# Eight columns of a graph kernel's edge lists: from one-hot products to GpSimd gathers

## The chip, the cores and the metric

The kernel runs on one core of a Trainium2 chip. The metric is the device time of one execution in microseconds. The engines are TensorE (PE), VectorE (DVE), ScalarE (ACT), GpSimd (POOL) and SyncE (SP). Each works through its own instruction queue, and semaphores order them against each other.

## The reference, cut to what matters

There are 3125 nodes with 128 features and 103125 edges, sorted by destination (50000 random pairs in both directions, and a loop at each node). Four graph layers follow each other, each behind a layer norm and a ReLU:

```
x = x + L0(h)   # attention by 8 heads; the score adds a bias of the edge's type
x = x + L1(h)   # GAT convolutions (the kernel's three "conv" passes), leaky ReLU of e_src + e_dst, softmax
x = x + L2(h)   # attention with edge features and weights
x = x + L3(h)   # normalised sum over the neighbours
# what L0 and L1 do at each destination:
e     = score(src, dst)                      # L1: leaky_relu(e_src[src] + e_dst[dst])
w     = exp(e - segment_max(e, dst)[dst])
alpha = w / segment_sum(w, dst)[dst]
out   = segment_sum(h[src] * alpha, dst)
```

So every layer needs, for each edge, the source node's row (its projected features and, in L1, its score), and a softmax and a sum over the edges of one destination. The whole is computed in fp32.

## The kernel before, in words

The nodes, padded to 3200, are ordered by degree and cut into 25 blocks (NB) of 128 destinations, one destination to a partition. The edges of a block are taken in *runs* of up to 64 edges a partition. Here each block has one run, so that a pass has 25 runs, after one step ahead of the first. Block 0 holds the nodes of the highest degree.

An early stage (L1018 to L1165) sorts each run's sources into *columns*, one source row per partition in each:

- columns 0 to 24 (*narrow*): column c holds a source out of table block c. Column 25 holds a second one out of the last block.
- columns 26 to 33 (*wide*, NW = 8): each holds a further source out of three blocks.
- the rest, by falling key: the first eight (FIRST) always, and four (MORE) more for each *turn* that the run's fullest partition needs. The number of turns, at least one, stands in `rturn`.

`pieces(c)` (L104) gives the products of a column: one one-hot matrix with one table block for a narrow column, three for a wide one. It also writes the row numbers of the rest to `el_ovf` (L1252), and the places within a block to `el_loc`.

**Convolution pass** (`conv_pass`, L2607, three times). The table of source rows stands in SBUF as three bf16 pieces (L2767). For each run:

- DVE makes the one-hots out of `loc` (`onehots`, L2756): one instruction for 34 columns against `iota_p`, and two for the wide columns' second and third blocks.
- PE multiplies them with the table (`get_rows`, L2953), three products for each piece, three columns to a PSUM bank; ACT copies the banks to `rows` (`take_rows`, L2883) in twelve copies.
- POOL copies the row numbers (`gather_first`, L2702) and gathers eight columns into `land_a`, one indirect DMA a column; ACT copies them into `rows` (`take_landed`, L2892) and frees `land_a`.
- DVE weighs the 42 columns (`weigh`, L2786): scores, maximum, softmax weights with ACT's Exp, product, and a tree of sums. Then for each turn it does the same for four columns of `rows_r`.

POOL's order is, for run r: `gather_first` for run r+1, then the turns of run r (`gathers`, L2718): wait for `land_r_free`, copy the numbers, four indirect DMAs into `land_r`; then `keep_list`, and `store_rows`, which scatters the previous block's output rows. SP's order (L2680): `copy_overflow` for run r-2 of its counter, that is all turns of the run being weighed: wait for the turn's gathers and for `rows_r_free`, move `land_r` to `rows_r`, free `land_r`; only then `load_list` and `load_loc` for the run after the next. `run_idx` has one buffer, and so have `land_a` and `land_r`.

**Edge pass of L0** (`l0_pass`, L2031). It is alike, with keys and values apart. PE makes key columns in two halves of six banks: `early_keys` ahead of the run and the rest in it. The type bias of each of the 42 columns comes by three more products with `oht` (`type_rows`), and landed keys are added by an identity product out of `land_a` (L2531). Then come the value columns in twelve groups (`values`, L2550), while ACT copies the landed values to `va`. DVE multiplies the keys with the queries (L2302), reduces, makes the weights, multiplies the values (L2322, L2325) and sums. A turn needs eight indirect DMAs, four of them for the type rows.

The attention pass of L2 and the final sum (`sum_pass`) use the same early stage, but have their own lists and loops.

## Time and profile before

| | us |
|---|---|
| median of 3 runs (8163.74 to 8175.19) | 8171.97 |
| the profiled execution | 8224.43 |
| its span | 8222.7 |

| engine | busy us | share of the span | instructions |
|---|---|---|---|
| PE products | 3022.9 | 37% | 29723 |
| PE weight loads | 2454.6 | 30% | 29724 |
| DVE | 4813.4 | 59% | 11169 |
| ACT | 1435.3 | 17% | 3773 |
| POOL | 3490.1 | 42% | 3926 |

Busy time is the sum of an engine's instructions; register, branch and semaphore work is not in it. A POOL gather's entry is the time in which POOL makes the transfer, not the time until the rows land. In a timeline the brackets hold the idle time ahead of an instruction and what ended it; "POOLq L2706" means that POOL's own queue stood at the wait of line 2706. The mean granted clock of PE was 0.679 of full speed.

### The profile page before, as it was taken

The page shows a single profiled execution, that of the slowest core. Times are in us where ns is not written, and L with a number is a line of the kernel's source. Part 1 is how long each engine was busy: PE and PEld are TensorE (multiplying, and loading weights), DVE is VectorE, ACT ScalarE, POOL GpSimd, SP SyncE. Part 2 cuts the span into 40 slices and gives each one's busy share as a digit, 9 for nine tenths or more (in the row PEclk, how much of TensorE's full clock was granted, in tenths as well). Part 3 has the DMA queues.
Part 4 walks back from the last instruction along what each step waited for, and adds up shares of the span by engine and source line. Part 5 has one row for each costly group of instructions (what it writes and reads, how often), then busy time and mean ns, then how long its engine had stood idle before and what let it go on. Part 6 is the DMA issues. An engine that isn't in the chain of part 4 may idle for free. (4 is left out here: it accounts for less than half of the span.)

```text
span 8222.7 us, 115102 instructions
## 1 busy us (share of the span) xinstructions
PE 3022.9 (37%) x29723; PEld 2454.6 (30%) x29724; DVE 4813.4 (59%) x11169; ACT 1435.3 (17%) x3773; POOL 3490.1 (42%) x3926
## 2 busy tenths in 40 slices
PE   4189423445566652244323432344300000001344
PEld 3178312344455542233223432333200000000122
DVE  9658835556566555677556875677544444444333
ACT  0123100111111121222112221344411111110000
POOL 0100113333323324456445653544466665563655
PEclk9999955667677675667666676666655555555666
DMA  0023203333323333334433453334322222222334
GB/s 20 10 85 100 51 27 100 80 92 88 85 69 83 77 60 68 79 80 87 64 75 80 82 82 61 72 80 72 57 48 53 52 52 50 46 50 54 78 82 78
DMA packets 297357, 557.19 MB, mean 68 GB/s; under 512 B 137694, under 2 KB 182475, under 8 KB 280515
## 3 DMA queue, kind: packets, MB, share of 16 engines
q0 software_dynamic: 112432, 254.18, 20.4%
q1 hardware_dynamic: 146802, 260.29, 10.0%
q10 hardware_dynamic: 38049, 41.86, 1.7%
q8 instruction: 31, 0.51, 0.0%
q14 instruction: 43, 0.35, 0.0%
HBM read 459.57 MB, written 29.32 MB: 59 GB/s over the span
## 5 line engine op out<-in xcount | busy, mean ns | idle before, releaser
L2967 PE MATMUL bank<-tab,oh 128*128 128x136 bf16 x11700 | 895.5, 249 | 695.4 <-PEq L2959 406.5
L2967 PEld LDWEIGHTS bank<-tab,oh 128*128 128x128 bf16 x11700 | 866.2, 112 | 755.5 <-issue 755.5
L1382 PE MATMUL bank<-ident,hid 128*128 128x128 f32 x125 | 55.8, 446 | 2651.0 <-PEq L1381 1182.8
L1382 PEld LDWEIGHTS bank<-ident,hid 128*128 128x128 f32 x125 | 22.7, 182 | 2697.7 <-issue 2697.7
L2710 POOL DMA_INDIRECT land_a<-table,idx_a x624 | 680.2, 1090 | 228.9 <-issue 166.4
L2729 POOL DMA_INDIRECT land_r<-table,idx_r x492 | 495.8, 1008 | 215.6 <-issue 144.4
L2546 PE MATMUL bank<-tab_l,oh_l 128*128 128x128 bf16 x3846 | 446.8, 243 | 289.2 <-issue 230.7
L2890 ACT ACTIVATE rows<-bank 128x408 f32<-128x408 f32 x936 | 398.5, 513 | 854.3 <-ACTq L2889 639.5
L2816 DVE TENSOR_TENSOR prod<-prod 128x128 f32<-128x128 f32 (+4 forms) x621 | 536.8, 864 | 14.6
L2519 PE MATMUL bank<-rel_l,oht_l 128*128 128x128 bf16 x3222 | 436.8, 261 | 245.4 <-issue 124.6
L2802 DVE TENSOR_TENSOR prod<-rows,bank 128x5376 f32<-128x5376 f32 x75 | 431.6, 5755 | 53.5 <-DVEq L2801 30.6
L2302 DVE TENSOR_TENSOR kp_l<-bank,own 128x512 f32<-128x512 f32 (+1 forms) x300 | 179.0, 622 | 442.0 <-DVEq L2301 370.6
L3193 PE MATMUL bank<-tab_l,oh_l 128*128 128x384 bf16 x1250 | 265.7, 383 | 455.4 <-PEq L3187 339.6
L1691 POOL DMA_INDIRECT table<-stage,stage_i x150 | 220.7, 1471 | 467.9 <-POOLq L1690 455.3
L2546 PEld LDWEIGHTS bank<-tab_l,oh_l 128*128 128x128 bf16 x3846 | 297.3, 109 | 355.4 <-issue 354.6
L1597 DVE TENSOR_TENSOR kk<-work_l,bank 128x512 f32<-128x512 f32 x232 | 159.5, 687 | 402.4 <-issue 197.3
L2519 PEld LDWEIGHTS bank<-rel_l,oht_l 128*128 128x128 bf16 x3222 | 288.0, 119 | 318.4 <-issue 318.4
L1877 POOL DMA_INDIRECT land_a<-table,idx_a x312 | 297.2, 953 | 115.8 <-issue 80.9
L1877 POOL DMA_INDIRECT land_b<-table,idx_b x312 | 296.7, 951 | 114.9 <-issue 101.8
L1877 POOL DMA_INDIRECT land_c<-table,idx_c x304 | 288.9, 950 | 111.0 <-issue 90.0
L3193 PEld LDWEIGHTS bank<-tab_l,oh_l 128*128 128x128 bf16 x1250 | 137.6, 112 | 583.4 <-issue 528.9
L2161 POOL COPY idx_a_l<-run_idx_l 128x8 int32<-128x8 int32 x26 | 12.7, 490 | 680.8 <-POOLq L2160 680.8
(506 smaller groups left out, 8264.3 us busy)
## 6 DMA issues: line engine op xcount, KB each, us to landing
loc<-el_loc SPq DMA_DIRECT2D x78, 1088.0 KB
loc_l<-el_loc SPq DMA_DIRECT2D x52, 1088.0 KB
rows_r<-land_r SPq DMA_DIRECT2D x123, 272.0 KB
landings_l<-landings_l SPq DMA_DIRECT2D x41, 784.0 KB
attr<-in_edge_attr ACTq DMA_DIRECT2D x75, 343.8 KB
land_a<-table,idx_a POOLq DMA_INDIRECT x936
typ_l<-el_typ SPq DMA_DIRECT2D x52, 192.0 KB
land_r<-table,idx_r POOLq DMA_INDIRECT x492
```

Source lines behind the costliest of these rows:

```text
L1691: pool.indirect_dma_start(target, bass.IndirectOffsetOnAxis(ap=stage_i[0:rows].bitcast(U32), axis=0), stage[0:rows], None).then_inc(s("tab ...
L1877: pool.indirect_dma_start(rows_of(x, h, width)[:, n, :], None, source, bass.IndirectOffsetOnAxis(ap=idx[x][:, c:c + 1].bitcast(U32), axis= ...
L2302: scores = dve.tensor_tensor(kp[:, of[0]:of[0] + len(of), 0:D], keys_of(n)[:, 0:len(of)], slots(blk(own0, b, 0, D), len(of)), ALU.mult)
L2519: done = pe.matmul(to, oht[:, i], rel3[:, k, x], start=first and x == 0, stop=last and x == 2, skip_group_check=True)
L2546: pe.matmul(keys_of(n)[:, c - of[0]], oh[:, o], tab[:, t, x, 0:D], start=m == 0 and x == 0, stop=False, skip_group_check=True)
L2710: pool.indirect_dma_start(land_a[:, c, :], None, source, bass.IndirectOffsetOnAxis(ap=idx_a[:, c:c + 1].bitcast(U32), axis=0)).then_inc(s( ...
L2729: pool.indirect_dma_start(land_r[:, c, :], None, source, bass.IndirectOffsetOnAxis(ap=idx_r[:, c:c + 1].bitcast(U32), axis=0)).then_inc(s( ...
L2802: dve.tensor_tensor(prod[:, 0:n].rearrange("p s (h d) -> p s h d", h=HEADS), of[:, :, 0:D].rearrange("p s (h d) -> p s h d", h=HEADS), wt[ ...
L2816: dve.tensor_tensor(prod[:, 0:half], prod[:, 0:half], prod[:, half:2 * half], ALU.add).then_inc(ch.semaphore, ch.one())
L2890: act.activation(rows[:, g * BANKC:g * BANKC + m].rearrange("p s w -> p (s w)"), got[g % full][:, 0:m * W1], ACT.Copy).then_inc(s(f"bank_f ...
L2967: last = pe.matmul(got[g % full][:, (c - of[0]) * W1:(c - of[0] + 1) * W1], oh[:, o], tab[:, t, x], start=n == 0, stop=n == len(parts) - 1 ...
L3193: last = pe.matmul(ps_sum[k], oh[:, o], tab[:, t].rearrange("p x d -> p (x d)"), start=n == 0, stop=n == len(half) - 1)
```

## The change

In the edge pass and the convolutions the wide columns are no longer made by one-hots. The eight wide sources of each partition are gathered by POOL, with the eight that it gathers already. The columns are now FC = 26 narrow ones and LAND = 16 landed ones, 42 as before. The early stage still chooses narrow, wide and rest columns as it did, and writes the row numbers of the wide ones ahead of the others, so that the turns hold the same edges.

```diff
-        el_ovf = dram("el_ovf", [RMAX + 1, P, 2 * LISTW], I32)
+        el_ovf = dram("el_ovf", [RMAX + 1, P, NW + 2 * LISTW], I32)
...
-  sp.dma_start(el_ovf[bass.ds(r + n, 1)]..., ov_i[:, PC:])
+  sp.dma_start(el_ovf[bass.ds(r + n, 1)]..., ov_i[:, PC - NW:])
# l0_pass
+            FC = NB + 1
+            LAND = MC - FC
-            wide = [range(c, min(c + 4, PC)) for c in range(NB + 1, PC, 4)]
-            landed_groups = [range(PC + c, PC + c + HALF) for c in range(0, FIRST, HALF)]
-            key_groups = landed_groups + wide + narrow
-            value_groups = [range(max(c - BANKC, 0), c) for c in range(PC, 0, -BANKC)]
+            landed_groups = [range(c, c + HALF) for c in range(FC, MC, HALF)]
+            key_groups = landed_groups + narrow
+            VG = 2 * len(banks)
+            value_groups = [range(FC * (n - 1) // VG, FC * n // VG) for n in range(VG, 0, -1)]
# both passes: SP loads fewer places; the edge pass loads the types in two DMAs, not four
-  sp.dma_start(loc[:], el_loc[bass.ds(r, 1), 0:PC]...)
+  sp.dma_start(loc[:], el_loc[bass.ds(r, 1), 0:FC]...)
# both passes: POOL
-  pool.tensor_copy(idx_a[:], run_idx[:, 0:FIRST])
+  pool.tensor_copy(idx_a[:], run_idx[:, 0:LAND])
-  for c in range(FIRST):
+  for c in range(LAND):
       pool.indirect_dma_start(land_a[:, c, :], None, source, ...idx_a[:, c:c + 1]...)
# both passes: DVE
-  dve.tensor_scalar(oh[:, 0:PC]..., loc[:], iota_p[:], None, ALU.is_equal)
-  for k in range(1, WIDE):
-      dve.tensor_scalar(oh[:, PC + (k - 1) * NW:PC + k * NW]..., iota_k[:, k:k + 1], None, ALU.is_equal)
+  dve.tensor_scalar(oh[:]..., loc[:], iota_p[:], None, ALU.is_equal)
# conv_pass
-  columns = [range(g, min(g + BANKC, PC)) for g in range(0, PC, BANKC)]
+  columns = [range(g, min(g + BANKC, FC)) for g in range(0, FC, BANKC)]
-  act.wait_ge(s(f"got_a{number}"), r * (16 * FIRST) + 16 * FIRST)
-  act.activation(rows[:, PC:], land_a[:], ACT.Copy)
+  act.wait_ge(s(f"got_a{number}"), r * (16 * LAND) + 16 * LAND)
+  act.activation(rows[:, FC:], land_a[:], ACT.Copy)
```

In the edge pass the landed keys are now four groups of four columns, and DVE's product of the landed values (L2325) covers sixteen columns. The final sum reads its list from word NW of `el_ovf` on.

## Rows read from the trace of the kernel before

**Rows 1.** Stretches: busy us (instructions) by engine, PE clock, DMA share, GB/s.

```profile
1228.00:3075.00 1847.00, 1025.04 (x11172) 844.46 (x11172) 1045.68 (x1640) 255.76 (x734) 594.49 (x679) 0.69 0.34 81
3075.00:4922.00 1847.00, 650.84 (x7950) 602.05 (x7950) 1255.04 (x2480) 421.69 (x1142) 969.21 (x1031) 0.67 0.41 78
4922.00:5932.00 1010.00, 399.01 (x4025) 327.79 (x4025) 667.25 (x1372) 363.04 (x974) 459.81 (x518) 0.65 0.38 70
```

**Rows 2.** The same view, first convolution, L2726 alone: xcount is turns.

```profile
3121.60:3195.90 74.30, 3.59 (x5) 0.61 0.29 47
3195.90:3341.90 146.00, 2.19 (x9) 0.62 0.36 71
3341.90:3567.80 225.90, 3.52 (x12) 0.67 0.37 77
3567.80:3951.20 383.40, 4.17 (x14) 0.72 0.47 85
```

**Rows 3.** Timeline (start us, us, engine, line) of POOL, first convolution, two turns.

```profile
3416.78 0.19 POOL L2707 COPY idx_a<-run_idx 128x8 int32<-128x8 int32 x1 [6.03 <-POOLq L2706]
3422.83 0.94 POOL L2710 DMA_INDIRECT land_a<-table,idx_a  x1 [0.30 <-issue]
3424.08 0.95 POOL L2710 DMA_INDIRECT land_a<-table,idx_a  x1 [0.31 <-issue]
3454.59 0.19 POOL L2707 COPY idx_a<-run_idx 128x8 int32<-128x8 int32 x1 [5.87 <-POOLq L2706]
```

**Rows 4.** Timeline of SP in the same run.

```profile
3452.53 0.34 SPq L2650 DMA_DIRECT2D run_idx<-el_ovf  x1
```

**Rows 5.** Timeline of DVE in the same run.

```profile
3452.24 0.19 DVE L2789 TENSOR_TENSOR sc<-rows_r,own 128x32 f32<-128x32 f32 x1 [6.63 <-DVEq L2843]
```

**Rows 6.** Timeline of POOL, first convolution, a run of one turn.

```profile
3676.27 0.19 POOL L2707 COPY idx_a<-run_idx 128x8 int32<-128x8 int32 x1 [3.99 <-POOLq L2706]
3684.88 1.19 POOL L2710 DMA_INDIRECT land_a<-table,idx_a  x1 [0.30 <-issue]
3686.38 1.96 POOL L2710 DMA_INDIRECT land_a<-table,idx_a  x1 [0.30 <-issue]
3703.77 0.19 POOL L2707 COPY idx_a<-run_idx 128x8 int32<-128x8 int32 x1 [3.99 <-POOLq L2706]
```

**Rows 7.** Timeline of SP in that run.

```profile
3700.76 0.34 SPq L2650 DMA_DIRECT2D run_idx<-el_ovf  x1
```

**Rows 8.** Timeline of ACT in that run.

```profile
3702.37 1.10 ACT L2894 ACTIVATE rows<-land_a 128x1088 f32<-128x1088 f32 x1
```

**Rows 9.** Lines of the edge pass: busy, mean ns, idle before and releaser.

```profile
L2302 DVE TENSOR_TENSOR kp_l<-bank,own 128x512 f32<-128x512 f32 (+1 forms) x300 | 179.0, 622 | 442.0 <-DVEq L2301 370.6 <-issue 46.9 <-remote 24.0
L2322 DVE TENSOR_TENSOR kp_l<-bank,wt_l 128x408 f32<-128x408 f32 (+1 forms) x300 | 147.7, 553 | 52.8 <-DVEq L2321 49.8 <-remote 2.7
```

**Rows 10.** Timeline of DVE in that run of one turn.

```profile
3686.87 1.35 DVE L2759 TENSOR_SCALAR oh<-loc,iota_p 128x4352 bf16<-128x4352 f16 x1 [0.26 <-DVE sh L2795]
3688.13 0.88 DVE L2761 TENSOR_SCALAR oh<-loc,iota_k 128x1024 bf16<-128x1024 f16 x2
```

**Rows 11.** Timeline of PE, start of the first convolution.

```profile
3113.26 6.63 PE L2967 MATMUL bank<-tab,oh 128*128 128x136 bf16 x78 [0.72 <-PEq L2966]
```

**Rows 12.** Stretches of the third convolution, L2726 alone, as in rows 2.

```profile
5042.10:5193.60 151.50, 4.80 (x9) 0.61 0.34 68
5193.60:5427.30 233.70, 5.64 (x12) 0.65 0.37 74
5427.30:5856.30 429.00, 5.19 (x14) 0.69 0.43 77
```

**Rows 13.** Timeline of POOL, edge pass, a run of one turn.

```profile
2556.74 0.94 POOL L2185 DMA_INDIRECT landings_l<-rel_d,idx_r_l  x1 [0.30 <-issue]
2596.18 0.76 POOL L2161 COPY idx_a_l<-run_idx_l 128x8 int32<-128x8 int32 x1 [30.75 <-POOLq L2160]
```

**Rows 14.** Timeline of PE in the same run.

```profile
2558.92 0.26 PE L2546 MATMUL bank<-tab_l,oh_l 128*128 128x128 bf16 x1 [0.96 <-issue]
```

More of the change, by code:

```diff
@@ L2077, in l0_pass @@
             assert sorted(c for of in key_groups for c in of) == list(range(MC))
-            assert sorted(c for of in value_groups for c in of) == list(range(PC))
+            assert sorted(c for of in value_groups for c in of) == list(range(FC))
+            assert all(len(of) <= BANKC for of in value_groups)
             def keys_of(n):
@@ L2179, in gathers @@
                                 pool.sem_inc(s("land_r_free"), -1)
-                                pool.tensor_copy(idx_r[:], run_now[:].rearrange("p (k s) -> p k s", k=2)[:, :, bass.ds(i * MORE + FIRST, MORE)]).then_inc(ch.semaphore, ch.one())
+                                pool.tensor_copy(idx_r[:], run_now[:, NW:].rearrange("p (k s) -> p k s", k=2)[:, :, bass.ds(i * MORE + FIRST, MORE)]).then_inc(ch.semaphore, ch.one())
                                 copied()
@@ L2324, in main_chunk @@
                         onehots()
-                        dve.tensor_tensor(by_head(kp[:, PC:]), by_head(va[:]), wt[:, PC:MC].unsqueeze(3).broadcast_to([P, FIRST, HEADS, V]), ALU.mult).then_inc(ch.semaphore, ch.one())
+                        dve.tensor_tensor(by_head(kp[:, FC:]), by_head(va[:]), wt[:, FC:MC].unsqueeze(3).broadcast_to([P, LAND, HEADS, V]), ALU.mult).then_inc(ch.semaphore, ch.one())
                         dve.wait_ge(ch.semaphore, ch.count)
@@ L2706, in gather_first @@
                         pool.sem_inc(s("land_a_free"), -1)
-                        pool.tensor_copy(idx_a[:], run_idx[:, 0:FIRST]).then_inc(ch.semaphore, ch.one())
+                        pool.tensor_copy(idx_a[:], run_idx[:, 0:LAND]).then_inc(ch.semaphore, ch.one())
                         copied()
-                        for c in range(FIRST):
+                        for c in range(LAND):
                             pool.indirect_dma_start(land_a[:, c, :], None, source,
@@ L2725, in gathers @@
                                 pool.sem_inc(s("land_r_free"), -1)
-                                pool.tensor_copy(idx_r[:], run_now[:, bass.ds(i * MORE + FIRST, MORE)]).then_inc(ch.semaphore, ch.one())
+                                pool.tensor_copy(idx_r[:], run_now[:, bass.ds(i * MORE + LAND, MORE)]).then_inc(ch.semaphore, ch.one())
                                 copied()
@@ L2758, in onehots @@
                         dve.sem_inc(s("loc_in"), -16)
-                        dve.tensor_scalar(oh[:, 0:PC].rearrange("p c n -> p (c n)"), loc[:], iota_p[:], None, ALU.is_equal).then_inc(ch.semaphore, ch.one())
-                        for k in range(1, WIDE):
-                            dve.tensor_scalar(oh[:, PC + (k - 1) * NW:PC + k * NW].rearrange("p c n -> p (c n)"), loc[:, (NB + 1) * P:],
-                                              iota_k[:, k:k + 1], None, ALU.is_equal).then_inc(ch.semaphore, ch.one())
+                        dve.tensor_scalar(oh[:].rearrange("p c n -> p (c n)"), loc[:], iota_p[:], None, ALU.is_equal).then_inc(ch.semaphore, ch.one())
                         dve.wait_ge(ch.semaphore, ch.count)
@@ L2892, in take_landed @@
                     def take_landed(r):
-                        act.wait_ge(s(f"got_a{number}"), r * (16 * FIRST) + 16 * FIRST)
-                        act.activation(rows[:, PC:], land_a[:], ACT.Copy).then_inc(s("act_chain"), 1)
+                        act.wait_ge(s(f"got_a{number}"), r * (16 * LAND) + 16 * LAND)
+                        act.activation(rows[:, FC:], land_a[:], ACT.Copy).then_inc(s("act_chain"), 1)
                         act.wait_ge(s("act_chain"), 1)
```

71 lines of the change are left out of this document (33 added, 38 removed).

## The prediction

> **What bounds the kernel now.** The change touches four passes, so I read a table of stretches first. The edge pass takes 1847 us, the first two convolutions together 1847 us and the third 1010 us [rows 1]. In the convolutions no engine is busy throughout: over the first two, DVE works 1255 of 1847 us, POOL 969, PE 651 and ACT 422 [rows 1]. So I followed, in the timelines, who waits for whom in one run.
>
> A convolution makes 25 runs and one prefetch, and a run has 1, 2, 3 or 5 turns of four more landed columns. L2726 runs once a turn: in the first convolution 9 times over the three runs of 3 turns, 12 times over the six of 2, and 14 times over 14 runs of 1 [rows 2]. The first run has 5 [rows 2] and the last 1, which makes 41.
>
> In a run of 2 turns POOL copies the indices at 3416.78 and again at 3454.59: 37.81 us [rows 3]. Between them stand the eight gathers of the next run, one every 1.25 us (3422.83, 3424.08), then four gathers a turn. SP moves the second turn's rows and then issues the next list, at 3452.53 [rows 4], and POOL starts again when that list is in, 2.06 us later. DVE had waited 6.63 us for that same turn [rows 5]. This is a closed chain: list, eight gathers, turn gathers, landing, move, list. Only POOL, SP and the DMAs are on it, so its length is the run's length.
>
> In a run of 1 turn the same chain starts at 3676.27 and SP issues the list at 3700.76, +24.5 us [rows 6, 7]. With the same 2.06 us to land it would close at +26.55, but POOL starts at 3703.77, +27.50: it waits for the eight-column buffer, which ACT empties at 3702.37 + 1.10 = 3703.47 [rows 6, 8]. Here DVE and ACT set the time, and the POOL chain has 0.95 us to spare.
>
> The edge pass differs. There DVE waits 370.6 us in all for key banks from PE and 49.8 us for value banks [rows 9], and POOL works 594 of 1847 us [rows 1].
>
> **The change part by part.** Each run loses its eight wide columns. On PE that is 8 x 9 of 150 products in a convolution (78 stay), and in the edge pass 72 of 150 for keys and 72 of 150 for values. DVE loses the two extra one-hot instructions, and its main one shrinks from 34 to 26 columns. ACT loses three PSUM copies of 0.51 us and its landed copy doubles. POOL gains eight gathers a run, all in front of the turn gathers.
>
> *Convolutions, POOL.* Eight gathers at 1.25 us are +10.0 us [rows 3]. Something comes back: gathers beside DVE's one-hots are longer, 1.96 us at 3686.38 and 1.19 us before it where others take 0.95 [rows 6], with the one-hots at 3686.87 to 3688.13 + 0.88 = 3689.01 [rows 10]. The excess is 1.25 us a run. The new one-hots take 1.35 x 26/34 = 1.03 us instead of 2.14, so I take 0.6 us of it back and get **+9.4 us** a run (bounds: 8.8, all of it back, and 10.0, none). By the Trainium skill (SBUF — State Buffer, "SBUF: two separate sides") a GpSimd-issued DMA cannot write its descriptors while a vector instruction in a two-port mode holds the shared port, and the trace agrees; a lock that lasts as long as the instruction would return (2.14-1.03)/2.14 x 1.25 = 0.65 us a run.
>
> Behind POOL's longer gathering stand the turn gathers, SP's move, SP's next list and one-hot load, and the row scatter; DVE waits for the turn's rows.
> - Runs with 2, 3 and 5 turns lie on the chain already, so +9.4 us each: 10 runs, **+94 us** in each of the first two convolutions.
> - Runs with 1 turn go from 383.40/14 = 27.4 us [rows 2] to 26.55 + 9.4 = 35.95: **+8.5 us** x 14 = 119 us. What DVE, PE and ACT save there is worth nothing, because DVE's own 27.4 us then lie inside 36.
> - The last run of a pass ends in DVE's turn, not in a list. DVE can take the rows 0.29 us before SP issues the list [rows 4, 5], so its slack is over the chain's 0.95 us; I take 1.5: +8 us.
> - Before the first run PE has 78 products left after the last table tile (6.63 us) [rows 11], and 72 of those are wide ones. Some 4.5 us go, less than 6 because ACT's landed copy grows.
> - Sum for one of the first two: 94 + 119 + 8 - 4.5 = 216.5; both **+433 us**.
>
> *Third convolution.* ACT's work after each block stretches it: 429.00/14 = 30.6 us for 1 turn, 233.70/6 = 38.95 for 2, 151.50/3 = 50.5 for 3 [rows 12]. POOL's chain after the change is that of the first convolution: 35.95, 225.90/6 + 9.4 = 47.05, and 146.00/3 + 9.4 = 58.1 [rows 2]. The differences are 5.3 x 14 + 8.1 x 6 + 7.6 x 3 = 146, and with the first run (9.4), the last (some 4) and the start (-4.5) **+155 us**. All three: +588 us (bounds: with 10.0 a run +635, with 8.8 +543).
>
> *Edge pass.* POOL has room here: in a run of 1 turn it waited 30.75 us before its next list was used [rows 13]. So the gathers cost nothing directly, and the work ahead of the sum decides. DVE: one-hots -1.1 us; the value products stay at 42 columns a run, eight of them now landed and not out of PSUM, in one product more or less of the same size; -0.9 us a run as an estimate, -23 us. PE: 72 key products went in the early part, before DVE needs them, but the second half of the keys keeps all its 108 products, and it is for these that DVE waits. PE also stalls in a way no wait explains: at 2558.92 it issues one product after 0.96 us in which it waited for nothing that the profile shows [rows 14], one of some 25 such rows of that run, with one to three products each, and they end 2 us after POOL's last gather at 2556.74 [rows 13]. Elsewhere 78 products take 6.63 us, 0.085 us each [rows 11]. Fewer products leave less to stall; a gather stretch that is 10 us longer gives the stall more time. Bounds: every wait of DVE for banks gone, -(370.6 + 49.8) us [rows 9]; every run 10 us longer, +250 us. I take the middle of the two effects, nearest to no change: -23 from DVE and some -27 from value banks that come sooner (half of the 49.8), **-50 us**.
>
> *The rest.* Longer lists (eight words more) and shorter one-hot loads (26 columns of 34) lie beside other work: nothing. Build stage, attention pass and final sum do the same work.
>
> **Sum:** 588 - 50 = +538 us on the profiled execution of 8224.4 us (span 8222.7), so 8762 us there. The median without profile is 8171.97, 0.6% lower; carried over, **8710 us**.
>
> **The rivals.**
> - *A, the forecast:* POOL's gathers lengthen every convolution run. 8710 us. For it: rows 3 to 7.
> - *B, the edge pass gives back much more.* If the stall shrinks with the number of products, 144 fewer of 426 take a third or more of DVE's waiting and of what surrounds it: -250 us instead of -50, so 8510. For it: 370.6 us of waits. Against: 108 critical products stay. The Trainium skill (Runtime: NRT & Kernel Launch, "Instruction fetch mechanics") has engines stream their code in blocks and stall after jumps, and shorter loops need less of it; by that rule the change comes out near B. The instruction queues of the page carry next to nothing in this pass, so I do not follow it.
> - *C, the edge pass loses too.* The longer gathering keeps PE in its stall until DVE waits for keys 5 to 8 us more a run: +150 instead of -50, so 8910.
> - *D, the other side:* DVE sets the convolutions and POOL's gathers hide. Then a run saves DVE's 1.1 us (75 runs, -83) and the edge pass gives 200: 7890 us, faster. It decides if POOL has 10 us to spare before each list. Against it: 0.95 us spare in runs of 1 turn, none in those of 2 [rows 3, 6].
> - *E:* the change does what it says, but gathers in a row of sixteen queue up in the DMAs and cost 1.6 us each instead of 1.25: +2.8 us x 75, 8920.
>
> **How the numbers follow.** A 0.66, B 0.16, C 0.10, D 0.03, E 0.05. A alone spans 8610 to 8810: 45 us either way for the bounds of the convolutions, 55 for the edge pass. The range takes in the middle of B and half of the way to C and E: 8500 to 8860. A measurement of this kernel tells 0.2% (16 us) from no change. Faster by more 0.03, within 0.01, slower 0.96.
>
> **What would show it.** A: POOL's index copies L2707 some 36 us apart in runs of 1 turn and 47 in runs of 2, a DVE wait of 8 to 9 us for the turn's rows where none was in runs of 1, L2710 x1248, L2967 x6084 (78 x 78). The first two convolutions take some 2280 us instead of 1847 and the third 1165 instead of 1010. B or C: the edge pass well under 1750 or over 1900 us, with DVE's wait for key banks under 200 or over 450 us. D would show as POOL still waiting before L2707. The prediction is wrong if sixteen gathers take less than 16 us, or if the runs of 1 turn stay under 33 us.

## The result, and the profile after

The changed kernel takes 9041.96 us (median of 4 runs, 9035.46 to 9065.01) against 8173.58 us for the kernel before on the same chip: a ratio of 1.107, 95% interval 1.1048 to 1.1092, so 868 us slower. I had forecast 8710 us, 538 us slower, with a range of 8500 to 8860. The direction was right and the loss was far larger. The profiled executions differ by 9065.01 - 8224.43 = 841 us; the stretches below add up to 852 us, so the rest of the kernel has no part in it.

The page's head and its table of busy time. TensorE has a third fewer products, POOL works 804 us more.

```profile
span 9063.3 us, 96508 instructions
PE 2669.1 (29%) x20539; PEld 2042.5 (23%) x20540; DVE 4707.8 (52%) x10961; ACT 1450.9 (16%) x3539; POOL 4294.3 (47%) x4758
```

The stretches of [rows 1] (edge pass, first two convolutions, third), in the same columns:

```profile
1231.10:3199.50 1968.40, 849.09 (x7604) 673.96 (x7604) 1022.09 (x1587) 279.19 (x734) 782.40 (x888) 0.65 0.41 87
3199.50:5562.50 2363.00, 537.60 (x4206) 444.75 (x4206) 1201.69 (x2376) 420.99 (x986) 1350.02 (x1447) 0.55 0.34 67
5562.50:6787.20 1224.70, 334.68 (x2153) 243.28 (x2153) 638.56 (x1320) 356.13 (x896) 700.97 (x725) 0.56 0.33 64
```

Against [rows 1] the edge pass lost 121 us (forecast: a gain of 50), the first two convolutions 516 (forecast 433) and the third 215 (forecast 155). The forecast missed 171 us in the edge pass and 143 in the convolutions.

The turns of the first convolution, as in [rows 2] (5, 9, 12 and 14 turns; four gathers each, which is why the count is 20 to 56):

```profile
3238.80:3320.50 81.70, 19.40 (x20) 0.54 0.29 50
3320.50:3498.00 177.50, 34.86 (x36) 0.54 0.30 63
3498.00:3789.40 291.40, 46.25 (x48) 0.56 0.30 66
3789.40:4320.10 530.70, 53.28 (x56) 0.56 0.36 69
```

A run of 1 turn takes 530.70/14 = 37.9 us (forecast 35.95), one of 2 turns 48.6 (47.05), one of 3 turns 59.2 (58.1). POOL's timeline in a run of 1 turn, to set beside [rows 6]:

```profile
3940.17 0.19 POOL L2704 COPY idx_a<-run_idx 128x16 int32<-128x16 int32 x1 [4.93 <-POOLq L2703]
3947.52 0.95 POOL L2707 DMA_INDIRECT land_a<-table,idx_a  x1 [0.31 <-issue]
3948.77 1.68 POOL L2707 DMA_INDIRECT land_a<-table,idx_a  x1 [0.30 <-issue]
3957.02 0.94 POOL L2707 DMA_INDIRECT land_a<-table,idx_a  x1 [0.30 <-issue]
3958.26 2.75 POOL L2707 DMA_INDIRECT land_a<-table,idx_a  x1 [0.30 <-issue]
3961.32 1.22 POOL L2707 DMA_INDIRECT land_a<-table,idx_a  x1 [0.30 <-issue]
3977.73 0.19 POOL L2704 COPY idx_a<-run_idx 128x16 int32<-128x16 int32 x1 [5.31 <-POOLq L2703]
```

VectorE's timeline in the same run: the one-hots, the first additions of the tree, and the wait for the turn's rows.

```profile
3949.24 1.09 DVE L2756 TENSOR_SCALAR oh<-loc,iota_p 128x3328 bf16<-128x3328 f16 x1 [0.27 <-DVE sh L2789]
3957.24 4.48 DVE L2810 TENSOR_TENSOR prod<-prod 128x2688 f32<-128x2688 f32 x2
3975.35 0.19 DVE L2783 TENSOR_TENSOR sc<-rows_r,own 128x32 f32<-128x32 f32 x1 [11.19 <-DVEq L2837]
```

SP's timeline: the next list.

```profile
3975.66 0.34 SPq L2647 DMA_DIRECT2D run_idx<-el_ovf  x1
```

The chain is the one predicted: SP issues the list, POOL starts 2.07 us later, and VectorE, once the bottleneck of such runs, waits 11.19 us. Three gathers are long. One (1.68 us) lies beside the one-hots, as in [rows 6]. The other two (2.75 and 1.22) lie beside the tree of sums, which no gather of a run of 1 turn met before: the gathers then ended 17.9 us after the index copy and the tree began after them. What met the tree then was the row scatter, which nothing in the chain waits for; the trace of the kernel before already had its price, 3.67 us instead of the 1.02 that the scatter takes in the changed kernel:

```profile
3696.10 3.67 POOL L1691 DMA_INDIRECT table<-stage,stage_i  x1 [0.94 <-POOLq L1690]
```

The excess over 0.94 us is 0.73 + 1.81 + 0.28 = 2.8 us a run, where I had counted on 0.65.

The lines of both passes: POOL's gathers of a convolution, VectorE's waits there (346.5 before), and the waits for key and value banks of the edge pass, to compare with [rows 9].

```profile
L2707 POOL DMA_INDIRECT land_a<-table,idx_a x1248 | 1364.2, 1093 | 418.8 <-issue 356.0 <-POOLq L2697 61.9 <-POOLq L2722 0.9
L2783 DVE TENSOR_TENSOR sc<-rows_r,own 128x32 f32<-128x32 f32 x123 | 23.7, 192 | 1148.9 <-DVEq L2837 1148.9
L2296 DVE TENSOR_TENSOR kp_l<-bank,own 128x512 f32<-128x512 f32 (+1 forms) x300 | 179.0, 622 | 589.3 <-DVEq L2295 403.9 <-remote 98.2 <-issue 85.6
L2316 DVE TENSOR_TENSOR kp_l<-bank,wt_l 128x272 f32<-128x272 f32 (+1 forms) x300 | 121.2, 459 | 31.3 <-DVEq L2315 28.9 <-remote 2.0
```

VectorE's idle time ahead of its key products grew from 442.0 to 589.3 us although TensorE makes 1872 fewer key products. TensorE's timeline in an edge run of 1 turn that starts at 2566.06 shows why; POOL gathers from 2567.35 to 2598.12 and scatters until 2601.11. The rows are the end of a steady stretch, the first two and the last product of the stall, and the restart.

```profile
2582.73 0.49 PE L2540 MATMUL bank<-tab_l,oh_l 128*128 128x128 bf16 x3
2585.80 0.22 PE L2513 MATMUL bank<-rel_l,oht_l 128*128 128x128 bf16 x1 [2.58 <-issue]
2588.59 0.27 PE L2513 MATMUL bank<-rel_l,oht_l 128*128 128x128 bf16 x1 [2.58 <-issue]
...
2601.23 0.27 PE L2513 MATMUL bank<-rel_l,oht_l 128*128 128x128 bf16 x1 [2.55 <-issue]
2602.66 0.37 PE L2513 MATMUL bank<-rel_l,oht_l 128*128 128x128 bf16 x2 [1.16 <-issue]
```

For 20 us TensorE issues one product every 2.1 to 2.8 us and waits for nothing that the profile shows. The reader should compare the restart with POOL's last transfer: 2602.66 against 2601.11. Over the 13 runs of 1 turn from 2239.6 on, the last gap in front of a key product (counting those over 0.25 us) ends 35.3 to 35.5 us after the first gather; before the change the last gap of the stall ended at 23.2 to 23.3.

The stall also fell on other work. These are the first product of the second half of the keys and the first product of the landed keys, in the run of [rows 14] before the change and in the run above:

```profile
2567.72 0.48 PE L2546 MATMUL bank<-tab_l,oh_l 128*128 128x128 bf16 x3 [0.94 <-PEq L2508]
2590.09 1.44 PE L2519 MATMUL bank<-rel_l,oht_l 128*128 128x128 bf16 x12 [4.36 <-PEq L2508]
2579.68 0.48 PE L2540 MATMUL bank<-tab_l,oh_l 128*128 128x128 bf16 x3 [2.19 <-DVE kp_l L2296]
2622.30 0.83 PE L2513 MATMUL bank<-rel_l,oht_l 128*128 128x128 bf16 x12 [1.99 <-PEq L2502]
```

Before, in the steady runs of 1 turn, the stall hit the early keys and was over before the second half began. Now the early keys are out before it, and it takes the second half after 33 of its 108 products, the keys that VectorE waits for. And from the landed keys to POOL's next index copy, which waits for them, it is now 8.6 us (2622.30 to 2630.90) instead of 6.1 (2590.09 to 2596.18), because four groups of landed keys stand there instead of two.

The granted clock fell too, from 0.69 to 0.65 in this pass. In both kernels it is 0.50 (1.2 GHz) behind the stall, with three products every 0.32 us, and then 1.00, with three every 0.17 us. In the second half of the keys the slow stretch is about as long before (3.4 us, from 2567.72) as after (3.7 us, from 2602.82). So in these runs the clock is not what makes the difference.

### The profile page after: what moved, and what is told of

It reads as the page before. It is cut to its first block and busy times, and to the rows that moved or that the text cites. A ratio compares the mean times of both kernels' runs of the same rounds, so it can differ in the third digit from the quotient of the medians.

```text
span 9063.3 us, 96508 instructions
## 1 busy us (share of the span) xinstructions
PE 2669.1 (29%) x20539; PEld 2042.5 (23%) x20540; DVE 4707.8 (52%) x10961; ACT 1450.9 (16%) x3539; POOL 4294.3 (47%) x4758
## 5 line engine op out<-in xcount | busy, mean ns | idle before, releaser
L2707 POOL DMA_INDIRECT land_a<-table,idx_a x1248 | 1364.2, 1093 | 418.8 <-issue 356.0
L2961 PE MATMUL bank<-tab,oh 128*128 128x136 bf16 x6084 | 718.1, 300 | 822.5 <-issue 460.9
L2961 PEld LDWEIGHTS bank<-tab,oh 128*128 128x128 bf16 x6084 | 624.4, 137 | 940.8 <-issue 939.4
L2783 DVE TENSOR_TENSOR sc<-rows_r,own 128x32 f32<-128x32 f32 x123 | 23.7, 192 | 1148.9 <-DVEq L2837 1148.9
L2726 POOL DMA_INDIRECT land_r<-table,idx_r x492 | 497.1, 1010 | 216.6 <-issue 156.6
L2513 PE MATMUL bank<-rel_l,oht_l 128*128 128x128 bf16 x3222 | 401.2, 257 | 288.4 <-issue 234.5
L2296 DVE TENSOR_TENSOR kp_l<-bank,own 128x512 f32<-128x512 f32 (+1 forms) x300 | 179.0, 622 | 589.3 <-DVEq L2295 403.9
L2161 POOL DMA_INDIRECT land_a_l<-table,idx_a_l x416 | 407.2, 979 | 141.2 <-issue 119.4
L2884 ACT ACTIVATE rows<-bank 128x408 f32<-128x408 f32 (+1 forms) x702 | 316.8, 502 | 913.9 <-ACTq L2883 577.4
L2540 PE MATMUL bank<-tab_l,oh_l 128*128 128x128 bf16 x1974 | 297.7, 265 | 396.9 <-issue 266.0
L1877 POOL DMA_INDIRECT land_a<-table,idx_a x312 | 296.3, 950 | 116.5 <-issue 84.4
L1691 POOL DMA_INDIRECT table<-stage,stage_i x150 | 150.9, 1006 | 394.5 <-POOLq L1690 368.6
```

Of the source, the lines that this page charges most:

```text
L1877: pool.indirect_dma_start(rows_of(x, h, width)[:, n, :], None, source, bass.IndirectOffsetOnAxis(ap=idx[x][:, c:c + 1].bitcast(U32), axis= ...
L2161: pool.indirect_dma_start(land_a[:, c, :], None, source, bass.IndirectOffsetOnAxis(ap=idx_a[:, c:c + 1].bitcast(U32), axis=0)).then_inc(s( ...
L2296: scores = dve.tensor_tensor(kp[:, of[0]:of[0] + len(of), 0:D], keys_of(n)[:, 0:len(of)], slots(blk(own0, b, 0, D), len(of)), ALU.mult)
L2513: done = pe.matmul(to, oht[:, i], rel3[:, k, x], start=first and x == 0, stop=last and x == 2, skip_group_check=True)
L2540: pe.matmul(keys_of(n)[:, c - of[0]], oh[:, o], tab[:, t, x, 0:D], start=m == 0 and x == 0, stop=False, skip_group_check=True)
L2707: pool.indirect_dma_start(land_a[:, c, :], None, source, bass.IndirectOffsetOnAxis(ap=idx_a[:, c:c + 1].bitcast(U32), axis=0)).then_inc(s( ...
```

## The experiments

"Before" is the kernel before, "changed" the one after. A stretch is measured from POOL's first index copy of a pass to that of the next.

**e1, the convolutions alone.** The edge pass is the old function, its list read behind the eight new words:

```diff
-  sp.dma_start(run_idx[:], el_ovf[bass.ds(r, 1)]...)
+  sp.dma_start(run_idx[:], el_ovf[bass.ds(r, 1), :, NW:]...)
```

> The three convolutions of the changed kernel with the edge pass of the kernel before. Theory: the parts add, and the convolutions carry most of the loss. The convolutions of the changed kernel measure +731 us against those before (1846.4 to 2363 for the first two, 1010.1 to 1224.7 for the third), so some 8175 + 731 = 8905 us, with the edge pass back at 1847 us. Rival (the loss is shared, for instance the edge pass is slowed only beside changed lists): the convolutions stay under +650 us or the edge pass stays over 1900.

Measured 8918.67 us against 8165.75, ratio 1.092 [1.0901, 1.0938], +753 us. Edge pass and first two convolutions:

```profile
1230.20:3078.90 1848.70, 1038.13 (x11172) 848.87 (x11172) 1043.22 (x1639) 255.80 (x734) 592.25 (x679) 0.70 0.39 81
3078.90:5436.80 2357.90, 545.59 (x4206) 447.05 (x4206) 1201.60 (x2376) 421.13 (x986) 1348.20 (x1447) 0.56 0.34 67
```

**e2, the edge pass alone,** with the old `conv_pass` in the changed kernel.

> The edge pass of the changed kernel with the convolutions of the kernel before. Theory that the parts add: the edge pass takes 1968 us instead of 1847 and the convolutions what they took before, so some 8175 + 121 = 8296 us. Rival, my forecast's own step (the edge pass gives 50 us back, and the measured 1968 comes from what runs around it): about 8125 us.

Measured 8303.56 us, ratio 1.0163 [1.0146, 1.018], +138 us.

```profile
1230.00:3197.60 1967.60, 850.07 (x7604) 674.81 (x7604) 1020.52 (x1587) 279.23 (x734) 781.57 (x887) 0.65 0.41 87
3197.60:5038.70 1841.10, 655.57 (x7950) 606.97 (x7950) 1254.02 (x2480) 421.15 (x1142) 968.29 (x1031) 0.67 0.39 78
```

The parts add (753 + 138 = 891 against 868), and each loses by itself. So two separate errors of the forecast are to be explained.

**e3, the convolutions without the tree.**

```diff
-                        while n > 1:
+                        while n > 1 and first > 0:
```

> The changed kernel, with the tree of sums over the 42 columns (three kinds of additions of two SBUF tiles on VectorE) left out in the convolutions; the turns' trees stay. Theory that a VectorE addition of two SBUF tiles holds back a gather which wants its row numbers meanwhile: the gathers that take 2.75 and 1.22 us, 18 and 21 us after the index copy, take 0.94 again, the sixteen end at 21.6 us instead of 23.6, and a run of 1 turn takes 35.8 us instead of 37.8; some 75 x 2.0 = 150 us less, 8890 us. Rival (a long row of gathers fills a queue about its fourteenth, whatever VectorE does): these gathers stay long and the runs at 37.8 us, since VectorE waits 11 us there anyway; 9040 us.

Measured 8884.33 us (one run), 158 less than the changed kernel. POOL's gathers, the seventh and eighth of a row beside the one-hots, the last of the sixteen, and the next index copy; the row began with the copy at 3944.70:

```profile
3953.30 1.08 POOL L2707 DMA_INDIRECT land_a<-table,idx_a  x1 [0.30 <-issue]
3954.69 1.70 POOL L2707 DMA_INDIRECT land_a<-table,idx_a  x1 [0.30 <-issue]
...
3965.43 0.94 POOL L2707 DMA_INDIRECT land_a<-table,idx_a  x1 [0.30 <-issue]
...
3980.66 0.19 POOL L2704 COPY idx_a<-run_idx 128x16 int32<-128x16 int32 x1 [5.64 <-POOLq L2703]
```

The sixteenth ends 21.7 us after the copy instead of 23.6, the run takes 35.96 us, and no gather behind the one-hots is long. Over all three convolutions 156 us go. VectorE had waited 11 us in such a run, so the time it saves is not what shortens it (in a pass's last run, where VectorE ends, a part may be: it got 0.6 to 1.1 us shorter). The theory holds: an addition of two SBUF tiles holds back a gather that meets it. In the changed kernel's run above, the row of 4.48 us is two additions, the first until 3960.19 and the second until 3961.72, and the two gathers that met them ended 0.82 us behind the one and the other (3961.01 and 3962.54). The trace agrees with the Trainium skill (SBUF — State Buffer, "SBUF: two separate sides"), by which a vector instruction with both inputs in SBUF shuts out a GpSimd operation that reads SBUF until it ends; the gather issued at 3958.26, one microsecond into the tree, took 2.75 us.

**e4, eight gathers fewer in the edge pass.**

```diff
-                        for c in range(LAND):
+                        for c in of:        # range(NW, LAND), but all in the first step
```

> The changed kernel, with the eight gathers of the wide columns left out in the edge pass after the first step (their rows stay those of the first run); products, copies and sums are the changed kernel's. Theory that TensorE and the other engines are starved while POOL gathers: the last key product comes some 10 us sooner in a run of 1 turn (32 us after the index copy instead of 42), VectorE's wait for key banks falls from 404 us to under 200, and the edge pass from 1968 to 1720 to 1780 us, so 8800 to 8850 us. Rival (the slower keys come from the new order of the key columns, not from the gathers): the edge pass stays within 30 us of 1968, 9040 us.

Measured 8746.56 us (one run), 295 less. The pass, and VectorE's wait for key banks:

```profile
1229.80:2892.40 1662.60, 822.83 (x7604) 665.91 (x7604) 1014.88 (x1586) 279.25 (x734) 603.69 (x687) 0.68 0.42 87
L2296 DVE TENSOR_TENSOR kp_l<-bank,own 128x512 f32<-128x512 f32 (+1 forms) x300 | 173.5, 618 | 293.5 <-DVEq L2295 247.9 <-issue 36.8 <-remote 8.5
```

200 gathers cost 306 us here, 1.53 us each, more than POOL's own 1.25. The gain was beyond the expected one; the wait for key banks stayed over the 200 us expected. Without these gathers the pass is 184 us shorter than before the change: that is what some 3600 products fewer are worth, net of the longer landed keys.

**f1, plain DMAs for these eight gathers.**

```diff
+  if c < NW:
+      pool.dma_start(land_a[:, c, :], source[c * P:(c + 1) * P])...
+      continue
```

> The changed kernel; in the edge pass POOL issues for the eight wide columns plain DMAs of 128 consecutive table rows each instead of gathers by row number (same 128 x 1088 bytes, other rows, so the output changes). Leaving these gathers out had taken the pass from 1968 to 1663 us. Theory P (what starves the engines is the gathers as POOL makes them, not the bytes): the pass falls to 1663 to 1750 us, 8740 to 8830 us in all. Theory Q (it is the bytes or packets in the DMA engines): the pass stays over 1900 us, about 9000 us.

Measured 8873.62 us (one run), the pass 1788.3. Neither expectation: POOL spent 5 us on the eight instead of 10, and runs of 1 turn took 57.8 us (64.8 changed, 51.8 in e4). TensorE's last gap ended 24 us after the first of the gathers that were left, as in e4, but these started 5 us later. So the bytes as such do not cause it. Whether plain DMAs of POOL do so less than gathers stays open, because they ran while TensorE had few products due.

**f2, half the bytes.** The eight gathers fetch 512-byte rows of the small type table instead of 1088-byte rows.

```diff
+  if short and c < NW:
+      pool.indirect_dma_start(land_a[:, c, 0:D], None, rel_d, ...idx_t[:, c:c + 1]...)
+      continue
```

> The changed kernel; in the edge pass the eight wide gathers fetch 128 rows of 512 bytes (of the small type table) instead of 128 rows of 1088 bytes, in the same number (the output changes). Theory Q1, cost by bytes: of the 306 us that these gathers cost, (1088 - 512)/1088 go, 162 us: the pass takes some 1806 us, the kernel 8880. Theory Q2, cost by the number of gathers and packets: the pass stays within 30 us of 1968, 9040 us.

Measured 9054.71 us (one run); the pass took 1968.00 us against 1968.40, so the bytes of these gathers do not matter.

```profile
1230.20:3198.20 1968.00, 855.46 (x7604) 681.00 (x7604) 1015.65 (x1585) 279.21 (x734) 791.31 (x912) 0.65 0.40 80
```

**f3, TensorE's loop written out.**

```diff
-                    with pe.Fori(2, NB) as b:
+                    for b in range(2, NB):
```

> The changed kernel; TensorE's loop over the blocks of the edge pass is written out (23 times the same code in a row, no jump back), nothing else changes. Theory J: TensorE's stall after some 34 products of each run is the supply of its code after the jump back, slowed by POOL's gathers. Without the jump the last key product comes some 10 us sooner and the pass falls from 1968 to under 1850 us, 8920 or less. Rival S: code is supplied just as slowly without a jump, or the stall is not one of code: the pass stays within 40 us of 1968, 9040 us.

Measured 9049.53 us (one run), the pass:

```profile
1229.80:3196.80 1967.00, 861.31 (x7604) 682.40 (x7604) 1015.33 (x1586) 279.26 (x734) 787.42 (x887) 0.65 0.42 88
```

Theory J fell: the jump back has no part in it. By the Trainium skill (Runtime: NRT & Kernel Launch, "Instruction fetch mechanics") a taken branch can force a fetch before an engine goes on; no such cost shows in this comparison. The DMA view of the two kernels says more. From 1700 to 3180 us, a stretch of steady runs that each have the stall, the changed kernel's view lists the queues q0, q1 and q10 and no instruction queue at all; the written-out loop's view has these three and one line more:

```profile
q8 instruction: 53, 0.87, 0.2%
```

So TensorE stalls just as long in a kernel for which no code is fetched through these queues as in one for which 0.87 MB are.

**h1, fewer products in the keys:** the type products of the 26 narrow columns (18 in the second half) are left out.

> The changed kernel; in the edge pass the three products with the type matrix are left out for the 36 narrow key columns' (so 54 products in the second half of the keys instead of 108, and 54 fewer in the first half), the output changes. Theory N: TensorE can issue only a certain number of instructions (some 95 products' worth) from the start of a row of POOL gathers, and the rest trickles until the row ends. With half of the products it stays under that number: the last key product comes 22 to 30 us after the index copy instead of 42, and the pass falls from 1968 to 1600 to 1720 us. Rival T: from some 15 us into the row of gathers TensorE hardly issues, however few it has issued before: the last key product stays at 38 us or later, the pass over 1850.

The text on record has two counts wrong: there are 26 narrow columns, 8 of them in the first half, so 24 type products went there and 54 in the second. Measured 8999.99 us (one run), the pass 1890.5 us. The last key product came 37 to 38.5 us after the index copy, so theory N as I had put it fell and rival T's account fits: with so few products due TensorE stalled all the same, and its last gap ended 35.5 to 36.0 us after the first gather, as in the changed kernel. (This run, h2 and h3 were made on a chip on which the kernel before takes 8215 us, not 8174; their first two convolutions are within 4 us of the others', so the passes can be compared.) Only the products left to do behind the row were fewer.

**h2 and h3, POOL waits ahead of all gathers** until TensorE has issued the second half of the keys; h2 is the kernel before, h3 the changed one.

```diff
+  pool.wait_ge(s("keys_late"), 1)
+  pool.sem_inc(s("keys_late"), -1)
   gather_first()
   with pool.Fori(0, turns) as i:
...
   keys(groups_of_keys[AHEAD:])
+  pe.sem_inc(s("keys_late"), 1)
```

> The kernel before; in the edge pass POOL waits, ahead of its gathers, until TensorE has issued the second half of the run's keys. Theory that the gathers starve TensorE: the keys then come with no gathers beside them, VectorE's wait for key banks falls from 371 to under 150 us, a run of 1 turn from 61 to some 52 us (as with eight gathers fewer in the changed kernel), and the pass from 1847 to some 1700; 8020 us in all. Rival: the starving only moves to the value products and the early keys, or the later landing of the eight columns is waited for: the pass within 40 us of 1847 or above it, 8170 us or more.

> The same wait of POOL in the edge pass of the changed kernel, where 24 gathers stand in a row instead of 16. Theory: TensorE gets its keys out some 15 us sooner, but the gathers then end some 55 us after the run's start and the landed keys are late: the pass some 1800 us (1968 now), 8870 in all. Rival: the starving and the late landing take everything back: 1968 or more, 9040 us.

h2: 8177.11 us against 8215.13 on its chip, ratio 0.9958 [0.9944, 0.9972], the pass 1798.7 instead of 1847. h3: 9113.59 us (one run), the pass 2016. The second line is VectorE's wait for value banks in h2, 49.8 us before:

```profile
L2304 DVE TENSOR_TENSOR kp_l<-bank,own 128x512 f32<-128x512 f32 (+1 forms) x300 | 166.0, 616 | 55.3 <-DVEq L2303 55.0 <-issue 0.2
L2324 DVE TENSOR_TENSOR kp_l<-bank,wt_l 128x408 f32<-128x408 f32 (+1 forms) x300 | 152.7, 553 | 396.3 <-DVEq L2323 364.0 <-remote 27.7 <-issue 4.1
```

The key waits vanished as expected and the value waits took their place: the stall goes wherever the row of gathers is. h3 came out as its rival had it, 1968 us or more; why it lost and h2 won was not followed further than the row's length (31 us of gathers instead of 21).

**i1, a pause in the row.** As e4, with twelve tiny copies between the eight landed gathers and the turns'.

```diff
   gather_first()
+  for _ in range(12):
+      pool.tensor_copy(pause[:], run_idx[:, 0:1])...
+      copied()
   with pool.Fori(0, turns) as i:
```

> As e4 (the changed kernel, eight wide gathers left out of each run of the edge pass), and in their time POOL does twelve tiny dependent copies, some 10 us, between the eight landed gathers and the turns' gathers. So POOL's row ends about 33 us after the index copy as in the changed kernel, but with as few gathers as in e4. Theory G (the gathers themselves keep TensorE from issuing): the second half of the keys is issued in the pause, the last key product comes before 30 us (e4: 30.6; changed kernel: 42.4) and a run of 1 turn takes 50 to 57 us. Rival L (TensorE goes on when POOL's row of work ends, whatever POOL does in it): the last key product at some 42 us, the run at 62 to 65 us, the pass near 1968.

The copies took 4.5 us, not 10. Measured 8669.21 us (one run), 77 less than e4 although POOL does more; the pass 1563.3 instead of 1662.6. In runs of 2 turns the last key product came 16 to 17 us after the index copy instead of 29 to 30, and such a run took 57.8 us instead of 67.2. Runs of 1 turn stayed at 51.3 (51.8), with POOL's last gather at 27 us instead of 23. Rival L is out for both: in the run of 1 turn from 2278.07 TensorE issued keys without a gap while POOL copied, and over the 13 steady runs its last key product came 28.2 us after the index copy instead of 30.5, although POOL's row ended 4 us later. One part of L stands: in that run the last gap still ended 1.5 us behind the last gather. Two index copies of i1, a run of 2 turns apart:

```profile
1687.65 0.19 POOL L2159 COPY idx_a_l<-run_idx_l 128x16 int32<-128x16 int32 x1 [6.80 <-POOLq L2158]
1745.02 0.19 POOL L2159 COPY idx_a_l<-run_idx_l 128x16 int32<-128x16 int32 x1 [7.14 <-POOLq L2158]
```

**i3, eight gathers fewer in the convolutions,** the edit of e4 in `conv_pass`.

> The changed kernel with the eight wide gathers left out of each run of the convolutions after the first step (stale rows, the rest as changed). Theory of POOL's chain with the gathers that meet VectorE's tree: without them a run of 1 turn is no longer set by POOL, but by VectorE and ScalarE at 26 to 27 us (37.9 now), a run of 2 turns falls by 11 to 12 us to some 37 (48.6 now); the convolutions lose 730 to 780 us, the kernel takes 8260 to 8310. Rival (the products taken away did cost something, too, or the landed copy twice as large sets the run): runs of 1 turn over 29 us, less than 650 us in all.

Measured 8238.39 us (one run), 804 less, a little beyond the range. Runs of 1 turn took 26.4 us, of 2 turns 36.8. The first two convolutions:

```profile
3193.50:4985.30 1791.80, 430.94 (x4206) 380.52 (x4206) 1198.42 (x2376) 395.39 (x986) 892.44 (x1046) 0.61 0.38 73
```

600 gathers cost 804/600 = 1.34 us each, and the products, one-hots and PSUM copies taken away are worth 1847 - 1792 = 55 us in two passes (rows 1 of before).

**f4 and f5, the list handed on early** in the convolutions; f4 is the kernel before, f5 the changed one.

```diff
   # gather_first
   pool.tensor_copy(idx_a[:], run_idx[:, 0:FIRST])...
+  pool.tensor_copy(run_next[:], run_idx[:])...
   copied()
+  pool.sem_inc(s("list_free"), 1)
   # keep_list
-  pool.tensor_copy(run_now[:], run_idx[:])...
+  pool.tensor_copy(run_now[:], run_next[:])...
-  pool.sem_inc(s("list_free"), 1)
   # SP
-  copy_overflow(r - 2); load_list(r)
+  load_list(r); copy_overflow(r - 2)
```

> The kernel before; in the convolutions POOL copies the whole list aside as soon as it has it and frees its buffer, and SP issues the next list ahead of the turns' moves instead of behind them. Theory of the closed chain (list behind the moves, gathers behind the list): it opens, so runs of 2, 3 and 5 turns, which lie on it, get some 6 us shorter (2 turns: 37.65 to some 32 us, then set by VectorE), runs of 1 turn stay at 27.4; 10 runs x 6 us x 3 passes = 180 us less, some 7990 us. Rival (the turns themselves, their landing buffer and VectorE, set these runs, and the list only follows): no change, 8170 us.

> The changed kernel with the list of the convolutions handed on early, as it was done to the kernel before. There the runs of 2 turns fell from 37.65 to 35.8 us, where VectorE then works nearly without a break, and runs of 1 turn stayed at 27.5. Theory of the closed chain: here POOL has more to do than VectorE, and the chain is POOL's work and then some 5 us of landing, move, list and landing. Without these POOL goes on as soon as its scatter is issued, 33 us after the index copy in a run of 1 turn instead of 37.8, 43.5 instead of 48.6 with 2 turns: 24 runs x 5 us x 3 passes = 360 us less, 8680 us. Rival (the wait for the eight or sixteen columns' buffer, or the copies on ScalarE, set these runs): under 100 us less, over 8940 us.

f4: 8122.46 us against 8178.48, ratio 0.9932 [0.9914, 0.9949]; runs of 2 turns 35.9 us instead of 37.6, not the 32 expected. VectorE hardly waits in them now, so its own work was 35 us and the chain had only 1.7 us to give. The two turns of a run in f4:

```profile
3420.98 0.19 DVE L2791 TENSOR_TENSOR sc<-rows_r,own 128x32 f32<-128x32 f32 x1 [0.34 <-DVEq L2845]
3426.46 0.19 DVE L2791 TENSOR_TENSOR sc<-rows_r,own 128x32 f32<-128x32 f32 x1 [1.31 <-DVEq L2845]
```

f5: 8938.89 us against 8215.13, ratio 1.088 [1.0862, 1.0899]; against the changed kernel's 1.107 that is 1.9% of before, some 155 us, instead of the 360 expected. Runs of 1 turn fell to 35.1 us in the first two convolutions and rose to 42.8 in the third. Both theories missed it: the chain opened, but less was behind it than I had thought, and what lengthened the third was not followed.

**i2, f4 and h2 together; j1 and j2, the wait between the rows.** In j1 the wait of h2 stands between `gather_first()` and the turns' loop, on the kernel before with f4's convolutions; j2 has the changed edge pass instead.

> The kernel before with both reorderings that the experiments point to: in the convolutions the list handed on early (-56 us alone), in the edge pass POOL's wait for the second half of the keys (-38 us alone, -48 in the pass). Theory that they are independent: 90 to 105 us less than before, ratio 0.987 to 0.989, faster than both kernels. Rival: one takes from the other where the passes meet, less than 70 us.

> The kernel before with the list of the convolutions handed on early (as in i2), and in the edge pass POOL's wait for the second half of the keys between the eight landed gathers and the turns' gathers instead of ahead of both. i2, with the wait ahead of both, took 8065 us, its edge pass 1779, and VectorE waited 344 us for value banks: the stall had only moved to the value products. A pause of 4.5 us at this place had put the keys of runs of 2 and 3 turns out in one go (runs 9 us shorter than without it). Theory G (a short row of gathers is covered by what TensorE has in store, a long one is not): a run of 1 turn takes 50 to 56 us instead of 61, the pass 1600 to 1720 us, the kernel 7870 to 8000. Rival: value products stall as in i2, the pass within 40 us of 1779, the kernel 8040 to 8090.

> The same kernel as j1, but with the changed edge pass (26 columns by one-hots, sixteen landed). It tells whether the change pays in the edge pass once the gathers are split by the wait. For it: 144 fewer products a run, which took 8.5 us off what follows the row of gathers. Against it: eight gathers more in the first, uncovered row, 10 us a run. Theory G: the first row of sixteen ends 22 us after the index copy, the second half of the keys stalls from some 14 to 24 us, so runs are 2 to 6 us longer than in j1 and the kernel 50 to 150 us slower than j1. Rival (the saved products count more once the rows are split): not slower than j1.

i2: 8064.69 us against 8170.06, ratio 0.9881 [0.9861, 0.9901], 105 us less where the two alone gave 94. j1: 7922.87 against 8174.92, ratio 0.9704 [0.9687, 0.9722], faster than both kernels and the best found. j2: 8032.21, ratio 0.9834 [0.9814, 0.9855], 109 us behind j1; the ends of the two intervals are apart. The loss lies in the runs of several turns (70.9 us against 59.5 in j1 for 2 turns, 88.8 against 77.2 for 3). The 13 steady runs of 1 turn take 54.7 us against 56.7 in j1, not the 2 to 6 us more that theory G had, so in these the change pays once the row is broken. The edge passes of j1 and j2:

```profile
1227.00:2869.60 1642.60, 996.28 (x11172) 845.05 (x11172) 1048.34 (x1639) 255.69 (x734) 650.62 (x679) 0.74 0.37 91
1229.80:2962.20 1732.40, 827.67 (x7604) 676.53 (x7604) 1018.00 (x1586) 279.22 (x734) 828.26 (x888) 0.67 0.46 99
```

j1 makes the same products and gathers as i2 and f4, in other order, and the convolutions of the three are alike. Its edge pass takes 1643 us; with the whole row behind the second half of the keys (i2) it took 1779, and with POOL starting beside the keys as before (f4) 1833. POOL's timeline of a run of 2 turns in j1, the end of the first row and the start of the second, with 5 us of waiting between them, which ends as TensorE comes to its value products (the first at 1760.1):

```profile
1753.59 0.94 POOL L2164 DMA_INDIRECT land_a_l<-table,idx_a_l  x1 [0.30 <-issue]
1759.63 0.19 POOL L2182 COPY idx_r_l<-run_now_l 128x8 int32 x1 [5.09 <-POOLq L2181]
1760.61 0.97 POOL L2185 DMA_INDIRECT landings_l<-table,idx_r_l  x1 [0.79 <-POOLq L2154]
```

## Why the forecast was wrong

- **What bounds the convolutions: right.** POOL's closed chain sets every run, and VectorE's wait for a turn's rows went from 346.5 to 1148.9 us. Rival D is out: i3 gives runs of 26.4 us back as soon as the gathers go.
- **The price of eight gathers in the chain: a term of the wrong size.** I took 10.0 us less 0.6 us returned. The 10.0 held. What failed is the step "something comes back": I looked only at which VectorE instructions the old gathers met, not at which ones the new, later gathers would meet. Each row now reaches the tree and pays 2.09 us there, in runs of every length. (My reading of [rows 6, 10] was loose, too: the gather of 1.19 us ended at 3686.07, before the one-hots began at 3686.87.) Runs came out at 37.9 to 38.8 us for 1 turn against 35.95, and e3, without the tree, lies at 2267.5 + 1164.4 - 2857 = +575 us over before for the three passes, where the forecast was +588.
- **A smaller miss:** "some 4.5 us" before the first run were 6.8 (46.1 to 39.3).
- **The edge pass: the step that failed is "so the gathers cost nothing directly".** POOL had 30 us of room, and that room was real. But TensorE's stall, which I had seen and put at -420 to +250 us in bounds, is not one thing beside the gathers: it lasts as long as their row. Its last gap follows the row's end in every kernel whose keys lie beside the row (changed 35.3 to 35.5 us after the first gather, f2 35.4, f3 35.5, h1 35.5 to 36.0, e4 23.0 to 24.7, before 23.2). So a run of 1 turn is the row plus what the engines still have to do behind it: before 23.3 + 38.1 = 61.4 us, changed 35.3 + 29.5 = 64.8. The eight gathers, with the scatter now behind them in the same row, put 12.0 us on the first term. The second lost 8.6: from the restart to the last key product it is 5.5 us instead of 15.6, since with 72 early products fewer the projections and 33 of the 108 late ones now come ahead of the stall; some 2 of these 10 us go again behind the last key, mainly to the longer landed keys (8.6 us instead of 6.1 to the next index copy), which the forecast had not counted. Against B I had said "108 critical products stay". They did, and the stall, which in these runs had missed them before, now held them.
- **Rivals.** C named the mechanism and nearly the size (+150 forecast, +121 measured), and I gave it 0.10; of its two signs the pass over 1900 us came, and the wait for key banks over 450 us did not (403.9, with 589.3 of idle time in all). B is out with the pass's 1968 us, and its rule on jumps with f3. E is out for the convolutions: its 1.6 us a gather is not what the rows show, since all but three of the sixteen are 0.94 to 1.07 us long. (Its sum was also short: 0.35 us more on each of sixteen gathers are 5.6 us a run, not 2.8.)
- **The tests that I had named:** 36 and 47 us between index copies (37.9 and 48.6 came), a wait of 8 to 9 us for the turn's rows (11.19), 1248 gathers and 6084 products in the convolutions (as said), an edge pass over 1900 us for C (1968 came).

What stays open is why TensorE stalls. It is not a jump (f3), not the bytes of the gathers (f2), not POOL being at work as such (i1), and it begins only after TensorE has issued some tens of products since the first gather (44 to 88 before and 49 to 72 changed, up to the first gap over 0.6 us that no wait or projection explains). That had made me think of a store of instructions that is not refilled during a row of gathers. The trace speaks against it as far as code comes through the instruction queues, since in the changed kernel they bring nothing during these runs; what else holds TensorE back no run shows.

## What to carry to other kernels

When work is moved onto POOL's gathers, lay the new, longer row over the other engines' timelines: what it now lies beside counts, not what the old row lay beside. A row of gathers is not free because POOL has room. Put it where the busiest engine has nothing due, or break it with a wait: the same products and gathers took 1833 us with one row beside the keys (f4), 1779 with one row behind them (i2), and 1643 in two rows with a wait between (j1).

## What I had not expected of the hardware

- TensorE issued 7 products in 20 us while POOL gathered, with no wait on record, and ran on within 2 us of POOL's last gather or scatter; 512-byte rows did it as much as 1088-byte rows (1968.0 and 1968.4 us for the pass).
- A gather issued one microsecond into an fp32 addition of two SBUF tiles took 2.75 us instead of 0.94.
- A pause of 4.5 us in POOL's row made the kernel of e4 77 us faster (8746.56 to 8669.21).
- TensorE's stall was there, as long as ever, in a stretch of 1480 us for which the trace has no instruction fetch at all.
